# Attention scores kept in token order in PSUM, masked into borrowed SBUF, and put into groups of 32 by the exponential

## The reference

```python
h = _layernorm(x) * (1 + ca) + sa
latent_kv = h @ w_kv_down                      # 256 -> 128
k, v = split(latent_kv @ w_kv_up)              # 128 -> 16 heads x 64, each
q = h @ w_q
att = einsum('bqhd,bkhd->bhqk', q, k) * 64 ** -0.5
att = softmax(where(causal, att, -inf))
x = x + ga * (einsum('bhqk,bkhd->bqhd', att, v).reshape(...) @ w_out)
```

## Time and profile before

| | us |
|---|---|
| median of 3 runs | 1837.28 |
| the 3 runs | 1831.57, 1837.28, 1837.82 |
| the profiled execution, its time | 1832.37 |
| its span in the profile | 1830.9 |

### The profile page before, as it was taken

One profiled execution on the slowest core, in us unless ns is written; L12 is line 12 of the kernel. 1 busy time (PEld: TensorE's weight loads), 2 busy tenths in 40 slices (PEclk: granted clock), 3 DMA queues, 4 the chain that ended last, 5 costly groups with the idle time before them and its releaser, 6 DMA issues.

```text
span 1830.9 us, 41208 instructions
## 1 busy us (share of the span) xinstructions
PE 1745.9 (95%) x16374; PEld 1236.4 (68%) x16374; DVE 1257.9 (69%) x2775; ACT 894.8 (49%) x1970; POOL 854.3 (47%) x1282
## 2 busy tenths in 40 slices
PE   7899999998999999999999999999999999999998
PEld 4666785767567667566856777756775667765667
DVE  5788857625788884762678888575367888667445
ACT  5577725232477763422357676332245767543223
POOL 2677743131177774222127777424113777731410
PEclk9899999999999999999999999999999999999999
DMA  8555540141355553022135555304014555420500
GB/s 236 123 137 142 118 149 1 27 67 37 83 132 126 132 119 127 1 49 45 36 108 130 129 125 118 110 1 85 9 39 130 129 125 128 113 93 1 93 1 25
DMA packets 119343, 163.76 MB, mean 89 GB/s; under 512 B 30224, under 2 KB 86256, under 8 KB 118128
## 3 DMA queue, kind: packets, MB, share of 16 engines
q1 hardware_dynamic: 105712, 154.83, 35.3%
q10 hardware_dynamic: 13440, 6.30, 1.2%
HBM read 62.44 MB, written 4.24 MB: 36 GB/s over the span
## 4 chain that ended last, share of the span: by engine, by line
PE 81%; DVE 7%; SPq 5%; ACT 3%; issue 1%; DMA 1%; POOL 1%; DVEq 0%; POOLq 0%
PE bank L661 13%; PE scores L641 12%; PE scores L450 11%; PE bank L450 7%; PE bank L702 5%; SPq L978 3%; PE bank L708 3%; PE bank L704 3%; PE scores L1719 2%; PE scores L1632 2%; PE scores L1086 2%; SPq L347 2%; PE scores L421 2%; PE scores L1155 2%; PE scores L1139 1%; PE scores L1274 1%
## 5 line engine op out<-in xcount | busy, mean ns | idle before, releaser
L866 POOL COPY placed<-prob 32x768 f32<-32x768 f32 x384 | 315.4, 821 | 27.5
L287 POOL TENSOR_TENSOR rstd<-rstd,minus_half 128x2 f32<-128x2 f32 x96 | 69.8, 729 | 543.1 <-DVE rstd L286 542.5
L905 ACT ACTIVATE prob<-prob,neg_max 128x768 f32<-128x768 f32 (+5 forms) x384 | 273.6, 714 | 97.3 <-DVE neg_max L787 97.3
L661 PEld LDWEIGHTS bank<-placed,v_t 128*64 128x64 f32 x4608 | 252.1, 138 | 75.9 <-issue 75.9
L661 PE MATMUL bank<-placed,v_t 128*64 128x128 f32 x4608 | 275.0, 276 | 17.3 <-DMA placed<-prob 12.8
L641 PE MATMUL scores<-k_t,q_t 64*128 64x128 f32 (+10 forms) x2176 | 287.9, 410 | 0.0
L795 DVE STREAM_TRANSPOSE prob<-prob 128x1536 f32<-128x1536 f32 x128 | 223.0, 1765 | 21.4 <-ACT prob L905 21.1
L641 PEld LDWEIGHTS scores<-k_t,q_t 64*128 64x128 f32 x2176 | 165.2, 187 | 71.7 <-issue 60.2
L787 DVE CUSTOM_DVE_ANT_1 prob<-scores,hx 128x128 f32<-128x128 f32 (+4 forms) x320 | 165.3, 576 | 46.1 <-PE scores L641 42.5
L854 POOL COPY rec_wide<-rec 128x128 f32<-128x128 f32 x256 | 65.0, 289 | 247.9 <-DVE rec L799 179.2
L866 POOL COPY placed<-hx 32x768 f32<-32x768 f32 x192 | 157.7, 821 | 13.7
(11 more groups left out here) (256 smaller groups left out, 3268.3 us busy)
## 6 DMA issues: line engine op xcount, KB each, us to landing
placed<-prob SPq DMA_DIRECT2D x640, 96.0 KB, 2.2
f<-in_L_ffn_f SPq DMA_DIRECT2D x16, 2048.0 KB, 13.5
placed<-hx SPq DMA_DIRECT2D x320, 96.0 KB, 2.1
x<-in_L_attn_x SPq DMA_DIRECT2D x8, 512.0 KB, 4.4
mod_rows<-mod_scratch SPq DMA_DIRECT2D x32, 128.0 KB, 5.6
out<-x SPq DMA_DIRECT2D x16, 256.0 KB, 2.1
w_ring<-in_L_attn_w_q ACTq DMA_DIRECT2D x24, 128.0 KB, 2.4
w_ring<-in_L_attn_w_kv_up ACTq DMA_DIRECT2D x48, 64.0 KB, 2.0
```

The lines of the kernel that those rows point to most:

```text
L287: step = pool.do(lambda e, ts=ts: nc.gpsimd.tensor_tensor(rstd[:, ts], rstd[:, ts], minus_half[:, ts], op=ALU.pow), var, filled)
L661: last = nc.tensor.matmul(out_bank[rows_, at_:at_ + P], v_t[pair % 2][:, j, rows_], placed[m % 2][:, :, head, first_block(m, i) + j, :], s ...
L866: nc.gpsimd.tensor_copy(placed[m % 2][target * GROUP:(target + 1) * GROUP, source, :, :, :], prob[m % 3][source * GROUP:(source + 1) * GRO ...
L905: nc.scalar.activation(p_, p_, ACT.Exp, scale=-1.0, bias=neg_max[:, k:k + 1], accum_out=row_sum[:, k:k + 1]).then_inc(flow["exp_done"], 1)
```

## The change

- **Natural order in PSUM.** `k_t` holds the keys in token order. A product is cut only at banks: round A has 5 products for each head in place of 7, round C has 4 in place of 7, round B has 3 as before.
- **Masked into borrowed SBUF.** `minimum` writes each head's masked scores contiguously: head 0 to `mod_rows[:, 2:8]`, head 1 to `x[:, 2:8]` (1536 columns each). There is one such buffer for each head, used by every round.
- **Permuted by the exponential.** It reads the borrowed buffer in runs of 32 keys and writes `prob[m % 3]` in the grouped order. The wait for `prob` (moves and copies of round m - 3) is now ahead of the first exponential of a round, on ACT.
- **Loads.** At the beginning of a sequence only tiles 0 and 1 of x and rows 0 and 1 are loaded (`EARLY = 2`); in the first sequence, SP loads rows 0 and 1 in rounds 8 and 9. The other tiles of x (2 DMAs, 256 KB and 512 KB) and the other 6 rows are loaded by SP behind the moves of the last round, in the first sequence too. The residuals wait for them by two new semaphores (`x_late`, `rows_late`). From the second sequence on, DVE waits ahead of the first `minimum` until the outputs of the previous sequence are stored, as it now overwrites x.
- The first copy of the raw modulations in the first sequence lies in `mod_rows[:, 0:2]` and a part of `tmp` in place of `mod_rows[:, 0:3]`.

```diff
+    EARLY = 2
+    LATE_X = ((EARLY, TH), (TH, T))
...
         def load_batch(e):
             e.wait_ge(stored, b * STORES + 16)
-            load_x(e, x, b, "x")
-            return load_rows(e, b)
+            e.dma_start(x[:, 0:EARLY, :], x_in[b][:, 0:EARLY, :]).then_inc(loaded["x"], 16)
+            return load_rows(e, b, range(EARLY))
...
+        masked_scores = [a[:, EARLY:T, :].rearrange("p t n -> p (t n)") for a in (mod_rows, x)]
...
-                        last = nc.tensor.matmul(score_tiles[head][:, at_ // 512, at_ % 512:at_ % 512 + count],
+                        last = nc.tensor.matmul(score_tiles[head][:, at_ // 512, at_ % 512:at_ % 512 + hi - lo],
                                                 q_t[buf][rows_, tile * P:(tile + 1) * P],
-                                                k_of[buf][rows_, groups, lo:hi], start=True, stop=True)
+                                                k_t[buf][rows_, lo:hi], start=True, stop=True)
...
                 nc.vector.tensor_tensor_reduce(
-                    prob[m % 3][:, :, head, blocks, :].rearrange("p g n i -> p g (n i)"),
-                    src.rearrange("p (g m) -> p g m", g=GROUPS), future[:, :, (T - 1 - tile) * GROUP:],
-                    1.0, BIG, op0=ALU.add, op1=ALU.min, accum_out=neg_max[:, k:k + 1]).then_inc(flow["masked"], 1)
+                    masked_scores[head][:, cols], score_tiles[head][:, :, :].rearrange("p a n -> p (a n)")[:, cols],
+                    future[:, (T - 1 - tile) * P:], 1.0, BIG, op0=ALU.add, op1=ALU.min, accum_out=neg_max[:, k:k + 1]).then_inc(flow["masked"], 1)
...
             for m in range(ROUNDS):
-                if b * ROUNDS + m > 2:
-                    moved, count = all_moved(m - 3)
-                    e.wait_ge(flow[moved], count)
-                    e.wait_ge(flow["kept"], base["kept"] + len(COPIES) * (m - 2))
+                if b and m == 0:
+                    e.wait_ge(stored, b * STORES + 16)
...
                 elif j[0] == "k":
-                    last = nc.scalar.copy(keys_half(pair % 2, half), by_group(ps))
+                    last = nc.scalar.copy(k_t[pair % 2][:, cols], ps)
...
             def exponential(m, i, head):
-                p_ = prob[m % 3][:, :, head, blocks_in(m, i), :].rearrange("p g n i -> p g (n i)")
                 k = column_of(m, i, head)
+                if i == 0 and head == 0 and b * ROUNDS + m > 2:
+                    moved, count = all_moved(m - 3)
+                    e.wait_ge(flow[moved], count)
+                    e.wait_ge(flow["kept"], base["kept"] + len(COPIES) * (m - 2))
                 e.wait_ge(flow["masked"], base["masked"] + part_number(m, i, head))
-                nc.scalar.activation(p_, p_, ACT.Exp, scale=-1.0,
+                nc.scalar.activation(prob[m % 3][:, :, head, blocks_in(m, i), :],
+                                     masked_scores[head][:, columns_in(m, i)].rearrange("p (n g i) -> p g n i", g=GROUPS, i=GROUP),
+                                     ACT.Exp, scale=-1.0,
                                      bias=neg_max[:, k:k + 1], accum_out=row_sum[:, k:k + 1]).then_inc(flow["exp_done"], 1)
...
+            for lo, hi in LATE_X:
+                e.dma_start(x[:, lo:hi, :], x_in[b][:, lo:hi, :]).then_inc(loaded["x_late"], 16)
+            load_rows(e, b, range(EARLY, 8), "rows_late")
...
-            read = dve.do(lambda e: nc.vector.tensor_tensor(a, ps, gate, op=ALU.mult), done, prior_x[slot], ROWS, X_LOADED)
-            wrote = dve.do(lambda e: nc.vector.tensor_tensor(x[:, t, :], x[:, t, :], a, op=ALU.add), read, *deps)
+            read = dve.do(lambda e: nc.vector.tensor_tensor(a, ps, gate, op=ALU.mult), done, prior_x[slot], ROWS,
+                          rows_late)
+            wrote = dve.do(lambda e: nc.vector.tensor_tensor(x[:, t, :], x[:, t, :], a, op=ALU.add), read,
+                           X_LATE if t >= EARLY else X_EARLY, *deps)
```

More of the change, by code:

```diff
@@ L191, in build @@
     loaded = {k: semaphore(f"loaded_{k}") for k in (
-        "weights", "wdown", "cond0", "wmod0", "cond1", "v1", "x_low", "x_high", "x", "next_x", "rows", "f1", "f2", "w0", "w1")}
+        "weights", "wdown", "cond0", "wmod0", "cond1", "v1", "x_low", "x_high", "x", "x_late", "next_x", "rows", "rows_late", "f1", "f2", "w0", "w1")}
     stored = semaphore("stored")
@@ L261, in build, with load_rows @@
     ROW_OF = ((0, 2), (0, 5)) + tuple((1, s) for s in range(6))
-    def load_rows(e, b, which=range(8)):
+    def load_rows(e, b, which, sem="rows"):
         for k in which:
@@ L563, in pieces_of @@
         def pieces_of(m, i):
-            at_, width, pieces = first_block(m, i) * P, (tiles_in(m)[i] + 1) * GROUP, []
-            for g in range(GROUPS):
-                start = at_ + g * width
-                edge = min(start + width, (start // 512 + 1) * 512)
-                whole = edge == start + width
-                if whole and pieces and pieces[-1][2:] == (0, width) and pieces[-1][0] // 512 == start // 512:
-                    pieces[-1] = (pieces[-1][0], slice(pieces[-1][1].start, g + 1), 0, width)
-                else:
-                    pieces.append((start, slice(g, g + 1), 0, edge - start))
-                    if not whole:
-                        pieces.append((edge, slice(g, g + 1), edge - start, width))
+            at_, end, key, pieces = first_block(m, i) * P, (first_block(m, i) + tiles_in(m)[i] + 1) * P, 0, []
+            while at_ < end:
+                edge = min(end, (at_ // 512 + 1) * 512)
+                pieces.append((at_, key, key + edge - at_))
+                at_, key = edge, key + edge - at_
             return pieces
@@ L579, in last_bank, with columns_in @@
             return ((first_block(m, i) + tiles_in(m)[i] + 1) * P - 1) // 512
+        def columns_in(m, i):
+            blocks = blocks_in(m, i)
+            return slice(blocks.start * P, blocks.stop * P)
         def out_slot(m, tile):
@@ L620, in batch @@
         MOD_CHUNKS = [(l, at_) for l in range(2) for at_ in range((1 - l) * MOD_CHUNK, 6 * D, MOD_CHUNK)]
-        mod_raw = mod_rows[:, 0:3, :].rearrange("p k n -> p (k n)")
+        mod_raw = [mod_rows[0:MOD_ROWS, 0:2, :].rearrange("p k n -> p (k n)")[:, q * P:(q + 1) * P] for q in range(QR)]
+        mod_raw.append(tmp[0:MOD_ROWS, 2, P:2 * P])
         MODS = 2 * 6 * C * NB
@@ L635, in scores @@
                 ends = {piece[1] // 512: piece[1] for piece in pieces}
-                for tile, at_, groups, lo, hi in pieces:
-                    count = (groups.stop - groups.start) * (hi - lo)
+                for tile, at_, lo, hi in pieces:
                     if m > 1 and at_ // 512 == SCORE_BANKS - 1:
@@ L1012, in batch, with residual @@
         prior_x = carry["prior_x"]
[L1014 removed]
+        def residual(t, ps, done, gate, *deps, slot=None, rows_late=ROWS_LATE):
             if gate is None:
@@ L1091, in head_output @@
             done = pe.do(last_product(ps, t), y_ready(t))
-            read, wrote = residual(t, ps, done, mod_rows[:, 0, :], slot=SPARE_TMP)
+            read, wrote = residual(t, ps, done, mod_rows[:, 0, :], slot=SPARE_TMP, rows_late=None)
             banks.read_by(i, read)
```

37 lines of the change are left out of this document (14 added, 23 removed).

## The result

| | us |
|---|---|
| kernel before, median of 5 runs | 1833.33 (1827.97 to 1837.82) |
| changed kernel, median of 5 runs | 1823.90 (1821.29 to 1825.55) |
| ratio, 95% interval | 0.9947 (0.9929 to 0.9965) |
| profiled execution of the changed kernel | 1825.55, span 1824.1 |

The change makes the kernel faster by 9.4 us between the medians and by 0.53% by the ratio. The interval excludes no change; in us it reaches from 6 to 13. 1825.8 us (1818 to 1834) was forecast.

A forecast was written before the change was run, and what follows sets the result against it. PE's own stream was taken to bound the middle of each sequence. Savings of 2.9 us in each of four sequences (11.6, taken as 11.5) off the median 1837.28 gave 1825.8 us, range 1818 to 1834 (8 in 10).

The forecast's parts named there:

- What bounds the kernel, and the pieces: PE's stream sets mid-sequence pace; pieces under about 130 columns pay for loads: round A saves 0.13 us, C 0.30.
- 2.9 us a sequence from the first values on: Savings in rounds A and C after a sequence's first values: 2.9 us, 11.6 us over four sequences.
- Do the others keep up?: Mid-sequence moves have 0.5 to 2 us slack against 0.43 taken, so PE doesn't wait, or 0.1 us now and then.
- rival (a): PE waits for moves once more in every pair; 4 to 8 us saved, 1829 to 1833 us; chance 0.21.
- Nothing gained up to the first values: At a sequence's start no shortened product lies on the path, so 0 us gained; the values only wait longer.
- the wait at 508.38 is 0.3 us longer: Sign at the second sequence's first values: PE's wait for moves, 1.05 us before, grows by 0.3 us.
- The absolute time: Whole kernel: 1825.8 us, from the earlier median of 1837.28 less 11.5, which is 0.63% less.
- The exponential, put at nothing: On ACT, reading in runs of 32 costs 0 us, bounded by about 0.1 us a pair; 512 columns stay at 715 ns.
- rival (b): ACT's exponential reads runs of 32 badly: some 1.9 us a pair slower, 53 us in all, 1890 us; chance 0.03.
- The late loads, put at nothing: After the last round, x lands by 706 with 2 us of slack: 0 us, upper bound a few us.
- rival (c): x tiles land after 708; each us late costs 4 us in all, 3 late gives 1838 us; chance 0.04.
- Rival (d): More saved on PE by contiguous keys, or clock falls moving 2.6 us each way; two fewer falls give 1820; chance 0.06.

The follow-up runs named there:

- old cuts: Changed kernel with its score products cut at the widths of the kernel before (7, 3 and 7 pieces for each head): 1832.26 us, ratio 0.9989.
- wide cuts: Changed kernel with 7, 3 and 7 score pieces for each head as before, but none narrower than 128 columns: 1824.78 us, ratio 0.9944.
- price by width: Changed kernel with round A in twelve 128-column pieces for each head and round B's first 512 columns in eight of 64: 1845.68 us, single run.
- pair with blocks left out: Kernel before and changed kernel, each with two of a round's 16 blocks left out (eight moves, six copies): 1825.46 and 1814.45 us.

## Why the prediction was right

- **What bounds the kernel, and the pieces: right.** Scores to values take 2.79, 2.78 and 2.79 us, forecast "2.78 to 2.80"; a pair takes 25.07 us, forecast 25.06. The old cuts, the wide cuts and the price by width show that it is the narrow pieces and their couples of loads: 0.112 us against "0.11 or a little more".
- **2.9 us a sequence from the first values on, 11.6 in all: right where the moves are out of the way** (11.6 in the pair with blocks left out, 2.7 to 3.1 in each sequence).
- **With ten moves less of it arrived.** 9.4 us came between the medians and 9.1 in the rounds. The times alone can't tell 9.4 from 11.5, as the interval reaches from 6 to 13 us; the traces have 8.0 from the first values on, where the sum has 11.6. The step that was mis-sized is "Do the others keep up?": "PE still doesn't wait, or by 0.1 us now and then". In the middle of the sequences the changed kernel has five waits, of 0.23 to 0.56 us and 1.8 in sum, where the kernel before has one of 0.23; with the waits at the ends they grew by 3.3 us from the first values on.

  Two things scatter there. The last move of a round lands from 2.2 to 4.1 us after its issue (0.38 at 539.14: 2.85; 1.24 at 513.62: 3.34), and the ten issues take from 6.2 to 7.8 us (1.75 at 1119.48: 7.26, where 0.72 at 671.17 has 6.23). The prediction took one landing of 2.2 us and one slack of 1.8.

  How much of the 3.3 us is due to PE coming earlier, and how much to more late landings in that one execution (19 against 7 over 2.6 us, but 9 with the wide cuts), these traces don't separate. This is rival (a) in a mild form: by the times a fifth of the saving is missing, by this stretch of the two traces three tenths, where it had a quarter to two thirds, and the waits do not come in every pair.
- **Nothing gained up to the first values: roughly so.** The gain of that part is -0.6, +0.5, -0.1 and +1.3 us in the four sequences, 1.1 in sum. The sign "the wait at 508.38 is 0.3 us longer" did not come: the first wait of the second sequence fell from 1.05 to 0.61 us.
- **The absolute time** (1825.8 against 1823.9) came out closer than it deserves, by luck: the median of before that it started from (1837.28, 3 runs) fell to 1833.33 with 5, so 0.53% stands against the forecast 0.63%.
- **The exponential, put at nothing: right, and rival (b) did not come.** 1151 ns where 1150 stood, and 722 and 709 for the two heads where 715 stood for both. ACT's wait for `prob` costs it 0.08 us a round, and nothing that the rounds of the old cuts show.
- **The late loads, put at nothing: right, and rival (c) did not come.** x is issued from 693.15 us on and lands 5.5 us after issue at most, by 700. The residual of tile 2, the first that reads it, begins at 704.84 and waits for none of it, nor does any other in the trace:

```profile
693.15 1.13 SPq L975 DMA_DIRECT2D x<-in_L_attn_x  x2
```
```profile
704.84 0.42 DVE L1017 TENSOR_TENSOR tmp<-scores,mod_rows 128x256 f32<-128x256 f32 x1
705.30 0.42 DVE L1019 TENSOR_TENSOR x<-x,tmp 128x256 f32<-128x256 f32 x1
```
- **Rival (d) did not come.** Reading grouped keys costs nothing (the old cuts). The clock did what was feared in both directions: the 128 products of the earlier trace rows went from 6.55 to 3.95 us in the first sequence, and from 3.95 to 5.50 and 6.55 in the third and the fourth.

## What to carry to other kernels

In this kernel a product whose columns stream faster than its stationary operand loads is paid by the load (64 columns: 0.058 us lost for each couple of loads; 128 columns: 0.006). To find such pieces elsewhere, count the instructions in the trace (here two for each f32 product), and take the spacing of the loads where they run without a gap: pieces that stream in less are the ones to look at. Slack read from one typical round is not slack: take the late tail of the transfers and of their issues over all rounds, since a shorter stream meets it. And before work goes to an engine that looks half idle, add up its rounds in that stage; here seven copies on POOL gained some 6 us and eight lost 44.

## What was not expected of the hardware

- With ten moves from one queue the last landing is late often enough that giving the tenth move to POOL gains 5.6 and 5.7 us (medians) in the two kernels, although the pair's timeline shows PE without idle time.
- The lower clock comes and goes at the same place of the same program: the same 128 products took 3.95, 5.50 or 6.55 us, after a wait of 1.73 us in each of the three rows above. In the rounds the last three sequences, which run the same program, also differ by 1 to 2 us in one trace, but there the granted clock stays at 1.0 (2.4 GHz). In the trace of before, the sequences of 214.2, 213.8 and 215.5 us have 2.6, 2.2 and 3.9 us of waits for moves.
- Reading in runs of 32 and not contiguously costs ACT nothing that shows: 1151 against 1150 ns for 1024 columns. For PE the Trainium skill ("Advanced Engine Details and Errata", PSUM Cachelines) says that any non-contiguous access significantly slows matmuls; the section is on PSUM. No run here shows that for keys in SBUF: products that read up to four separate runs take the same time as contiguous ones (the old cuts).
